# Mixing products placed ahead of the value products, one gather moved up, and one packed index per tile in a four-layer residual kernel

## What is computed

```
x = x + attention(x)        # 8 query heads, 4 key heads of 64; new k, v are written into a paged
                            # cache (blocks of 16 rows); a window of 256 positions is read back
x = x + x @ w1[subject]     # one 64 x 64 matrix per batch, chosen of 8
x = x + x @ W_base.T + scaling * lora(x, adapter2)    # one of 4 adapters of rank 16 per batch
x = x + x @ W.T + scaling * lora(x, adapter3)         # one of 8 adapters of rank 16 per batch
```

## Time and profile before

| What | Value |
|---|---|
| median of 3 runs | 427.21 us (425.41 to 427.32) |
| the profiled execution's own time | 422.87 us |
| its span, first to last instruction | 421.1 us |
| granted TensorE clock | 1.0 (its upper level, 2.4 GHz) throughout |
| PE busy | 409.3 us, 97% of the span |
| VectorE / ScalarE / GpSimd busy | 308.1 / 240.8 / 258.2 us |
| one tile of the main loop, tile 1 to 2 on PE | 17.28 us |

### The profile page before, as it was taken

How to read it: one execution, slowest core, us unless ns; L and a number is a source line. 1 busy time by engine, 2 the same in 40 slices (tenths; PEclk the granted TensorE clock), 3 DMA queues, 4 the chain that set the end, 5 groups by cost and what they waited for, 6 DMA issues and landing times.

```text
span 421.1 us, 9975 instructions
## 1 busy us (share of the span) xinstructions
PE 409.3 (97%) x2942; PEld 315.8 (75%) x2942; DVE 308.1 (73%) x901; ACT 240.8 (57%) x611; POOL 258.2 (61%) x230
## 2 busy tenths in 40 slices
PE   5999999999999988999999999999999999999997
PEld 1586877888945566888787878878778778888776
DVE  3798768769478586967978779687786787967742
ACT  4383433433267465756767567666676666765741
POOL 3206775275579877777777777777767777662000
PEclk9999999999999999999999999999999999999999
DMA  6616565157584455656555656565565655653321
GB/s 177 218 51 195 170 179 182 53 168 260 157 267 119 149 148 149 180 154 175 163 138 166 169 161 165 140 180 156 147 177 141 171 160 137 186 144 99 109 69 61
DMA packets 74107, 65.15 MB, mean 155 GB/s; under 512 B 50277, under 2 KB 52453, under 8 KB 74055
## 3 DMA queue, kind: packets, MB, share of 16 engines
q1 hardware_dynamic: 55088, 38.09, 31.3%
q0 software_dynamic: 15456, 22.08, 19.7%
q10 hardware_dynamic: 3510, 4.35, 2.9%
HBM read 74.46 MB, written 11.93 MB: 205 GB/s over the span
## 4 chain that ended last, share of the span: by engine, by line
PE 82%; DMA 5%; DVE 4%; POOL 4%; issue 4%; ACT 1%; SPq 0%; POOLq 0%; DVEq 0%; ACTq 0%
PE banks L1151 37%; PE banks L1141 11%; PE banks L1315 11%; PE banks L1294 9%; PE banks L1331 4%; PE banks L1167 3%; PE banks L1354 3%; PE banks L1344 2%; DMA wpt_late<-newkv,idx_all 1%; DMA newkv<-kvo 1%; POOL q_roots L497 1%; POOL wpt_late L524 1%; POOL windows L524 1%; DMA windows<-newkv,idx_all 1%; DMA xt_s<-xt_dram 1%
## 5 line engine op out<-in xcount | busy, mean ns | idle before, releaser
L524 POOL DMA_INDIRECT windows<-kvrows_dram,idx_all x78 | 83.0, 1064 | 31.1 <-issue 24.0
L524 POOL DMA_INDIRECT windows<-newkv,idx_all x78 | 81.8, 1049 | 29.0 <-issue 22.6
L655 ACT ACTIVATE pt_s<-banks 112x384 f32<-112x384 f32 x128 | 56.0, 496 | 61.9 <-PE banks L1141 56.9
L649 ACT ACTIVATE prob<-prob,negmax 128x336 f32<-128x336 f32 x128 | 72.4, 566 | 24.4 <-DVE negmax L1011 24.4
L1011 DVE CUSTOM_DVE_ANT_0 prob<-banks,mask 128x336 f32<-128x336 f32 x128 | 57.4, 503 | 2.7 <-PE banks L1294 1.2
L1021 DVE TENSOR_SCALAR prob<-prob,rinv 128x336 f32<-128x336 f32 x128 | 47.1, 410 | 2.3
L1294 PE MATMUL banks<-kt_s,qt_s 64*128 64x336 f32 x256 | 44.8, 468 | 0.0
L1315 PEld LDWEIGHTS banks<-pt_s,windows 112*64 112x64 f32 x624 | 33.3, 136 | 13.4 <-issue 10.9
L1315 PE MATMUL banks<-pt_s,windows 112*64 112x128 f32 x624 | 42.7, 279 | 0.0
L1151 PE MATMUL banks<-wf_hi,x 128*128 128x512 f32 x120 | 41.1, 403 | 0.0
L1141 PE MATMUL banks<-ident_r,prob_w 128*112 128x128 f32 x384 | 40.4, 242 | 0.0
(11 more groups left out here) (222 smaller groups left out, 918.2 us busy)
## 6 DMA issues: line engine op xcount, KB each, us to landing
usel<-utab SPq DMA_DIRECT2D x64, 128.0 KB
xt_s<-xt_dram SPq DMA_DIRECT2D x16, 256.0 KB, 3.7
newkv<-kvo SPq DMA_DIRECT2D x16, 256.0 KB, 2.6
stage<-xtok_dram SPq DMA_DIRECT2D x16, 256.0 KB, 11.3
tsel<-ttab SPq DMA_DIRECT2D x64, 64.0 KB
out_dram<-xo ACTq DMA_DIRECT2D x15, 256.0 KB
windows<-kvrows_dram,idx_all POOLq DMA_INDIRECT x78
windows<-newkv,idx_all POOLq DMA_INDIRECT x78
```

Of the source, the lines that this page charges most:

```text
L524: P.indirect_dma_start(kv_s[i][:, c, :], None, newkv if new else kvrows, bass.IndirectOffsetOnAxis(ap=idx_all[:, new * CH + c, b:b + 1], a ...
L649: A.activation(pr, pr, ACT.Exp, bias=negmax[:, g:g + 1], scale=-1.0, accum_out=psum_p[b % 2][:, g:g + 1]).then_inc(S["exp_done"], 1)
L655: A.activation(pt_s[g][:], tb[g % 2][0:KP, 0:CH * 128].rearrange("p (c q) -> p c q", c=CH), ACT.Copy).then_inc(S["pt_ev"], 1)
```

## The change

It has three parts. On PE, `mix(t-1)` stands ahead of `values(k)` and no longer between its halves. On POOL, `gather(3, 1)` stands ahead of the wait on `comb_ev` and of `gather(4, 0)`; after that the order of gathers is as before, although it is now written out. On DVE and SP, the three indices of the two batches of a tile are packed into one number (`picks`); SP reads that number once a tile and takes the indices apart with register operations.

```diff
@@ SyncE, load_tile
                 after(sp, S["l1_mm"], t - 1)
+                both = sp.value_load(picks[0:1, t:t + 1], min_val=0, max_val=PICKS * PICKS - 1)
+                pick = [both % PICKS, both // PICKS]
                 for u in range(2):
-                    s = sp.value_load(subj_s[0:1, 2 * t + u:2 * t + u + 1], min_val=0, max_val=7)
+                    s = pick[u] % 8
...
                 for u in range(2):
-                    a2 = sp.value_load(ad2_s[0:1, 2 * t + u:2 * t + u + 1], min_val=0, max_val=NE2 - 1)
-                    a3 = sp.value_load(ad3_s[0:1, 2 * t + u:2 * t + u + 1], min_val=0, max_val=NE3 - 1)
-                    a23 = sp.value_load(pair_s[0:1, 2 * t + u:2 * t + u + 1], min_val=0, max_val=NE2 * NE3 - 1)
+                    a23 = pick[u] // 8
+                    a2, a3 = a23 % NE2, a23 // NE2
@@ GpSimd
-            for k in range(NB):
-                if k == 0:
-                    pool.wait_ge(S["comb_ev"], NE3 // 2)
-                    gather(4, 0)
-                    continue
-                if k + 2 < NB:
+            gather(3, 1)
+            pool.wait_ge(S["comb_ev"], NE3 // 2)
+            gather(4, 0)
+            pool.wait_ge(S["pv_mm"], 1)
+            gather(5, 0)
+            gather(4, 1)
+            for k in range(2, NB - 2):
+                if k > 2:
                     gather(k + 2, 1)
                 if k + 4 < NB:
                     pool.wait_ge(S["pv_mm"], k)
@@ VectorE, meta
-                link(V.tensor_copy(adf[:, 1, :], ad3_s[:]))
-                link(V.scalar_tensor_tensor(adf[:, 2, :], adf[:, 1, :], float(NE2), adf[:, 0, :], ALU.mult, ALU.add))
-                V.tensor_copy(pair_s[:], adf[:, 2, :]).then_inc(S["meta_ready"], 1)
+                V.tensor_copy(adf[:, 1, :], ad3_s[:])
+                link(V.tensor_copy(adf[:, 2, :], subj_s[:]))
+                link(V.scalar_tensor_tensor(adf[:, 0, :], adf[:, 1, :], float(NE2), adf[:, 0, :], ALU.mult, ALU.add))
+                link(V.scalar_tensor_tensor(adf[:, 2, :], adf[:, 0, :], 8.0, adf[:, 2, :], ALU.mult, ALU.add))
+                two = adf[:, 2, :].rearrange("a (t u) -> a t u", u=2)
+                V.scalar_tensor_tensor(picks[:], two[:, :, 1], float(PICKS), two[:, :, 0], ALU.mult, ALU.add).then_inc(S["meta_ready"], 1)
@@ TensorE
-                    values(k, 0)
                     if t >= 1:
                         mix(t - 1)
-                    values(k, 1)
+                    values(k)
```

More of the change, by code:

```diff
@@ L149, in build @@
         adf = sb("adf", [1, 3, NB])
-        pair_s = sb("pair_s", [1, NB], i32)
+        picks = sb("picks", [1, TILES], i32)
+        PICKS = 8 * NE2 * NE3
         pos = sb("pos", [128, TILES])
@@ L1303, in probs_t, with values @@
                 last.then_inc(S["pt_mm"], 1)
-            def values(b, p):
+            def values(b):
                 t, u = b // 2, b % 2
@@ L1309, in values @@
                     pe.wait_ge(S["wf_ev"], 1)
[L1310 to L1318, removed]
+                for p in range(2):
+                    pe.wait_ge(S["pt_ev"], 4 * b + 2 * p + 2)
+                    for c in range(CH):
+                        for h in range(2):
+                            g = 2 * p + h
+                            col = 256 * u + 128 * p
+                            last = mm(ob[64 * h:64 * h + 64, col:col + 128], kv_s[b % WINDOWS][:, c, 256 + 64 * g:320 + 64 * g],
+                                      pt_s[g][:, c, :], start=(c == 0), stop=(c == CH - 1))
+                last.then_inc(S["pv_mm"], 1)
             def project(t):
```

## The result

The median after is 433.73 us (4 runs, 432.38 to 437.32); in the same session the kernel before took 426.41 us. The ratio is 1.0185, 95% interval 1.0117 to 1.0253: slower by 1.2 to 2.5%. The profiled execution after took 432.38 us, its span is 430.6 us, 9.5 us over that of before.

A forecast was written before the change was run, and what follows sets the result against it. Gathers on POOL were taken to bound the kernel up to about 160 us, then PE alone. Terms -2.03 + 0.1 + 0 + 0.5 = -1.4 us gave 425.8 us against the median 427.21, range 423.6 to 428.0.

The forecast's parts named there:

- What bounds the kernel: Main loop: gathers on POOL set PE's pace up to about 160 us, behind that PE alone does.
- The packed index: SP and DVE: seven of eight reads go, SP off the path; earlier loads beside the gathers cost +0.5 us.
- The +0.5 us of traffic: Batch 4's gather: tsel and usel loads starting up to 2.43 us earlier delay its landing, 0.46 us, taken as +0.5.
- the cover on DVE: DVE: packing's two tiny operations hide before an instruction waiting 0.82 us for ScalarE; cost nothing, without cover 0.4 us.
- The mix: PE: joining the value products saves a break of 0.145 us a mix, 14 counted, 2.03 us.
- late x1: PE's earlier mix: x1 is 0.44 us early in tile 1, worst in tile 9; 0.1 us of waits in all.
- a sign of being wrong: Main loop: the forecast fails if a tile is not shorter; 17.28 us was to become 17.14.
- The gather: POOL and PE: batch 3's 1.38 us wait goes, batch 4's grows from 1.50 to 3.0 us.
- the sum is nothing: Keys of batches 3 and 4: the moved gather gains nothing in total as long as batch 4's landing stays.
- The skill's rule: usel loads, broadcast over 2, stay on two engines and hold back gathers; without it the sum could be -1.9 us.
- Rivals: Besides (e): forecast 425.2 to 426.3 (0.47), earlier gathers 423.1 to 424.9 (0.22), POOL wait 427.2 (0.13), PE break 427.8 (0.11).
- (e): PE's mixes: x1 late in all 15 tiles, 2.1 us lost, 429.4 us and above; chance 0.07.

The follow-up runs named there:

- e6: Kernel before with only an unused 64-byte tile added, so later tiles lie 64 bytes higher; 434.65 us, ratio 1.0201.
- e5: Whole change with the packed tile as large as the one it replaces, so later addresses stay, against the kernel before; 425.16 us, ratio 1.0005.
- e1: The moved mix on PE alone, against the kernel before; 426.12 us, ratio 1.0023.
- e7: Moved mix plus each usel load split into two loads of 16 rows, against the kernel before; 420.77 us, ratio 0.9886.
- e12: Kernel before with only the usel loads split into two of 16 rows; 422.66 us, ratio 0.9923.
- e1 to e6: Against before: mix alone 1.0023, gather alone 1.0008, packing alone 1.0244, packing at old tile size 1.0027, whole change at old tile size 1.0005, addresses shifted 1.0201.
- e11: Moved mix, packing at the old tile size and split usel loads, without POOL's swap, against the kernel before; 420.27 us, ratio 0.9867.
- e15: Kernel before with pair_s in a dead part of adf and every tile behind it 64 bytes lower; 433.44 us, ratio 1.0166.
- e8: Whole change, unpadded, plus usel loads split into two of 16 rows, against the kernel before; 421.72 us, ratio 0.9885.
- e2_gather: The moved gather on POOL alone, against the kernel before; 425.63 us, ratio 1.0008.

## Why the prediction was wrong, step by step

- **What bounds the kernel.** "Behind batch 4 ... PE alone does" was the gap. The waits of PE show who was late in one execution, not how near the next one is. The `usel` loads of a tile took 17.6 us and more from the first issue to the end, with 1.4 us to spare where it was least; SP's issues of up to 4.76 us were a sign of it.
- **The packed index: the step that failed.** "SP's own time isn't on the path: these loads are needed a tile later" is where the loss came in: the cost of this part was put at 0.5 us beside the gathers and at nothing for the loads themselves. The loads are on the path as soon as they lose 1.4 us. And the cost of the edit was counted in instructions, while what cost 2% was the size of its new tile, which moved the addresses of all later ones (e6: nothing else changed, 1.0201; e5: nothing but this undone, 1.0005). The +0.5 us of traffic and the cover on DVE could not show it.
- **The mix.** Mechanism and size were right: 1.33 us of scores, 1.09 and 1.47 as in the earlier trace rows, no late x1 over 0.2 us. In e5_after_pad the scores of tile 1 and of 13 tiles on, 177.00 and 400.04, give 17.16 us a tile against 17.29. What was not seen is that it takes PE to `usel` sooner (e1). In the profile after, a tile is longer than before, (407.32 - 177.58) / 13 = 17.67 us, with the waits for `usel` in it; the prediction had named that as a sign of being wrong. With the loads split the gain stays in the tile, 17.17 in e7 against 17.30 in e12; the intervals of their ratios overlap.
- **The gather.** As forecast the wait of batch 3 nearly went, POOL got no new wait, and batch 4 waited about 3 us (2.82). PE's new wait for `ot_lo` behind batch 3 was not seen, 0.36 us after. The landing took 6.25 us against 5.61, 0.64 more where +0.5 was put; but from the last piece to PE's start it's 5.06 to 6.89 us in the runs with unsplit loads that I compared (before, e1 to e6, after), so this nearness can be luck. Mis-sized was "the sum is nothing": behind one wait of 2.82 us PE takes 2.74 us more, at half clock, and e5_after_pad shows the same (wait 2.65, keys to scores 177.00 - 161.35 = 15.65 us).
- **The skill's rule.** The Trainium skill, "DMA: Bandwidth & Descriptors", section "Rules for kernel authors", keeps a load with an outermost repeat of 2 to at most 2 engines. The trace agrees: about 3 semaphore updates for each `usel` load against about 15 for one without the repeat, and without it the wait on `usel` and the wait at batch 4 both go (e7, e11). The prediction used the rule to back its 0.5 us beside the gathers, and not to ask how long two engines need for a tile's loads.
- **Rivals.** None had this end. The slower one, (e), 429.4 us and above (its own terms, 427.21 + 2.1, give 429.3), takes in the measured 433.73 but for another reason: x1 late in every tile, where no mix waited over 0.2 us. The range ended at 428.0.

The whole change with its addresses kept took 425.16 us, near the forecast 425.8, but that is partly luck: against its own kernel before the ratio is 1.0005 and not the forecast 0.997, and in its profile the 2 us of the mix are outweighed by 2.7 us at half clock, which the prediction did not have.

## What to carry to other kernels

Before pricing a cut on the busiest engine, ask of every load it consumes how long that load takes from issue to landing against the length of the loop, and read the issuing queue's own rows: an issue that takes several times its shortest is a sign to look there, though it doesn't tell how late the loads are (e6 and before have the same rows). When an edit changes the size of a tile, compare the addresses of all later tiles, and test the edit once with the old size kept. Two waits merged into one need not cost what they cost apart: here the clock fell behind the longer one.

## What the runs showed of the hardware

- 64 bytes of address, in either direction and with no other change to what runs, cost 1.7 to 2.0% (e6, e15), and nothing measurable when the loads have room (e8). The mean `usel` packet goes from 170.7 ns to 178.8 to 180.8, the median from 159 to 160.
- A load of 32 rows in which 16 are repeated kept PE waiting, two loads of the same bytes did not, and their semaphore updates went from about 3 to about 15 a load: issues of `usel` in e11_best, to set beside the two rows of before and after:

```profile
L418 SPq DMA_DIRECT2D usel<-utab x128: 320/369/1844, 147.4 to 398.5; - x128
```

- After a wait of 2.82 us TensorE was granted 0.50 of its clock, and full clock was back in the window from 171 us; after 1.38 and 1.50 us apart, before, it never fell, yet after a single 1.47 us in e2_gather it did (0.61 in the window from 160 us). The length of the wait alone doesn't decide.
